# A fused cross-attention and mixture-of-experts layer: heads dealt over both halves of the rows, and a reordered head of the program

## The reference

```python
x = x + tanh(g_xattn[0]) * xattn(layernorm(x), ctx_1024, ...)   # (32, 128, 128)
x = x + tanh(g_ffn[0]) * ffn(layernorm(x), ...)

# xattn: 16 heads of width 8
qkv, qkv_a = x @ Wqkv + bqkv, xa @ Wqkv_aux + bqkv_aux
dots, dots_aux = q @ k.T * scale, q @ ka.T * scale               # the same queries, two sets of keys
p, pa = softmax(dots), softmax(dots_aux)
out = (p @ v) * (1 - sigmoid(g)) + (pa @ va) * sigmoid(g)
return out @ Wo + bo

# ffn: 64 experts of width 64, the best 8 of each token by a grouped sigmoid router, and a shared expert
y = sum over e of w[:, e] * ((silu(x @ wg[e]) * (x @ wu[e])) @ wd[e])
return y + (silu(x @ Ws_gate) * (x @ Ws_up)) @ Ws_down
```

## Time and profile before

| | |
|---|---|
| median of 3 runs | 859.26 us (859.24 to 859.61) |
| the profiled execution | 859.58 us, its span 857.8 us |
| busy, share of the span | PE 96%, weight loads 75%, DVE 80%, ACT 66%, POOL 74% |
| mean granted TensorE clock | 0.985 of 2.4 GHz |
| DMA | 120.04 MB, mean 140 GB/s |

### The profile page before, as it was taken

One profiled execution on the slowest core, in us unless ns is written; L12 is line 12 of the kernel. 1 busy time (PEld: TensorE's weight loads), 2 busy tenths in 40 slices (PEclk: granted clock), 3 DMA queues, 4 the chain that ended last, 5 costly groups with the idle time before them and its releaser, 6 DMA issues.

```text
span 857.8 us, 20206 instructions
## 1 busy us (share of the span) xinstructions
PE 826.2 (96%) x6733; PEld 646.0 (75%) x6733; DVE 683.6 (80%) x1648; ACT 566.8 (66%) x964; POOL 637.3 (74%) x602
## 2 busy tenths in 40 slices
PE   4899999999999999999999999999999999999997
PEld 3477777777766678888888888878888888888885
DVE  6789999999897769769678877867966977876665
ACT  4388888888878665575576576557557557655554
POOL 2668888888854378877787786777777788778785
PEclk8599999999999999999999999999999999999999
DMA  4677786776652167447456554654654755546562
GB/s 119 173 169 173 178 183 155 187 169 170 160 126 51 53 152 169 120 111 184 117 142 147 131 142 125 154 135 109 163 139 111 171 130 134 149 116 150 137 138 58
DMA packets 108036, 120.04 MB, mean 140 GB/s; under 512 B 28560, under 2 KB 70352, under 8 KB 106496
## 3 DMA queue, kind: packets, MB, share of 16 engines
q1 hardware_dynamic: 105056, 118.23, 57.5%
q10 hardware_dynamic: 2880, 0.59, 0.4%
HBM read 103.55 MB, written 14.71 MB: 138 GB/s over the span
## 4 chain that ended last, share of the span: by engine, by line
PE 87%; DVE 5%; DMA 3%; issue 2%; SPq 1%; ACT 1%; POOL 0%; DVEq 0%; POOLq 0%
PE bank L1999 20%; PE bank L2000 20%; PE bank L2001 20%; PE bank L1336 7%; PE bank L1323 5%; PE bank L1294 3%; PE bank L1276 2%; PE bank L1344 2%; PE bank L1260 1%; PE bank L1357 1%; DVE mx L989 1%; PE bank L1270 1%; DMA cwb<-wts_scratch 1%; DMA stack_q<-nmaxT 1%; PE bank L1976 1%
## 5 line engine op out<-in xcount | busy, mean ns | idle before, releaser
L1676 POOL TENSOR_TENSOR hid<-act,cwb 128x512 f32<-128x512 f32 x264 | 424.0, 1615 | 126.4 <-DVE act L1903 69.1
L1729 ACT ACTIVATE silu<-bank 128x512 f32<-128x512 f32 x256 | 152.9, 597 | 190.7 <-PE bank L2001 189.9
L1903 DVE TENSOR_TENSOR act<-silu,bank 128x512 f32<-128x512 f32 (+1 forms) x264 | 180.5, 684 | 119.5 <-ACT silu L1729 78.7
L1999 PE MATMUL bank<-xhi,weights_hi 128*128 128x512 f32 x520 | 206.6, 397 | 0.0
L1911 DVE TENSOR_TENSOR hlo<-hid,hhi 128x512 fp32r<-128x512 f32 x256 | 197.5, 772 | 8.5 <-ACT hhi L1735 8.3
L2001 PE MATMUL bank<-xlo,weights_hi 128*128 128x512 f32 x520 | 204.2, 393 | 0.0
L2000 PE MATMUL bank<-xhi,weights_lo 128*128 128x512 f32 x520 | 203.9, 392 | 0.0
L1735 ACT ACTIVATE hhi<-hid 128x512 fp32r<-128x512 f32 (+1 forms) x264 | 164.8, 625 | 15.7 <-POOL hid L1676 13.1
L989 DVE TENSOR_REDUCE mx<-bank 128x4 f32<-128x512 f32 x240 | 156.0, 683 | 16.6 <-PE bank L1294 14.8
L786 ACT ACTIVATE prob<-bank 128x1024 f32<-128x1024 f32 x128 | 131.2, 1025 | 48.6 <-PE bank L1323 46.5
L2001 PEld LDWEIGHTS bank<-xlo,weights_hi 128*128 128x128 f32 x520 | 97.6, 188 | 22.0
(11 more groups left out here) (238 smaller groups left out, 1022.1 us busy)
## 6 DMA issues: line engine op xcount, KB each, us to landing
cwb<-wts_scratch SPq DMA_DIRECT2D x174, 384.0 KB, 5.4
stack_k<-k_scratch SPq DMA_DIRECT2D x30, 256.0 KB, 4.3
k_scratch<-parts_k SPq DMA_DIRECT2D x15, 384.0 KB, 3.4
stack_q<-q_scratch SPq DMA_DIRECT2D x30, 128.0 KB, 2.9
stack_k<-k_scratch SPq DMA_DIRECT2D x30, 128.0 KB, 5.2
q_scratch<-parts_q SPq DMA_DIRECT2D x15, 192.0 KB, 2.7
xin<-in_x_dram SPq DMA_DIRECT2D x16, 128.0 KB, 3.0
cin<-in_ctx_dram SPq DMA_DIRECT2D x16, 128.0 KB, 3.1
```

The costliest lines, as they stand in the source:

```text
L1676: pool.tensor_tensor(h_buf[k][:], a_buf[k][:], cwb[slot][:, q % GP, :], ALU.mult).then_inc(h_ok, 1)
L1729: act.activation(s_buf[k % RS][:], g_bank[k % 2][:], ACT.Silu).then_inc(s_ok, 1)
L1903: nc.vector.tensor_tensor(a_buf[k % RS][at], s_buf[k % RS][at], u_bank[k % 3][at], ALU.mult).then_inc(a_ok, 1)
L1999: nc.tensor.matmul(bank, w[0], mh, start=first, stop=False)
```

## The change

Heads are dealt out over the two halves: head h goes to row `h % 2 * 8 + h // 2` of the 16, so even heads lie in half 0 and odd heads in half 1. The weights of the query and key projections are reordered for it (`by_row`), and the units of the scores take rows in the order `S_ROW = (0, 8, 2, 10, 4, 12, 6, 14)`, so the two units of a round lie in opposite halves. In a round TensorE issues first the eight shifted scores of both units, alternating halves and banks, then the four scores, alternating too. `stack_there` is called in round 0 alone and waits for both halves.

The biases of the projections are loaded as rows (two DMAs in place of three of single elements), reordered by ScalarE (L739 in the new file), and turned by three matmuls (L1384, `turn_biases`) and a copy. At the start, ScalarE issues three of the four pairs of key loads of chunk 0 (`load_first_k(act, ...)`), SP the others; the scores of a batch of chunk 0 wait for both halves; the first of them stand ahead of the transposes of chunk 2 on TensorE. The third split of chunk 1 moves from VectorE to GpSimd; GpSimd's clearing of the second V comes earlier, VectorE's `gate_consts` later.

```diff
-S_HEAD = (8, 10, 12, 14, 0, 2, 4, 6)
+S_ROW = (0, 8, 2, 10, 4, 12, 6, 14)
+ROW_OF = tuple(h % 2 * (H // 2) + h // 2 for h in range(H))
...
+    def load_first_q(eng, c, half):
+        wait(eng, q_first, 32)
+        eng.wait_ge(stack_clear, 2)
+        load_products(eng, q_of(0)[PARTS_AT[half]:PARTS_AT[half] + ROWS_S, :, c].rearrange("p h t -> p (h t)"),
+                      q0_v[c], False, half, HH * P, stk0[half][c])
+
+    def load_first_k(eng, c, half):
+        wait(eng, k_first[c], 16)
+        eng.wait_ge(stack_zero, 2)
+        load_products(eng, k_of(0)[PARTS_AT[half]:PARTS_AT[half] + ROWS_S, :, c].rearrange("p h a t -> p (h a t)"),
+                      k0_v[c], True, half, 2 * HH * P, stk0[half][c])
...
-        turned = lambda a: a.rearrange("(h d a) -> d h a", d=DH, a=1)
-        for i, b in enumerate((turned(v["bqkv"][0:P]), turned(v["bqkv"][P:2 * P]), turned(v["bqkv_aux"][P:2 * P]))):
-            sp.dma_start(bcol[:, i:i + 1], b, allow_slow_non_contiguous=True).then_inc(c_in, 16)
+        sp.dma_start(brow_in[:, 0:2 * P], one(v["bqkv"][0:2 * P])).then_inc(c_in, 16)
+        sp.dma_start(brow_in[:, 2 * P:3 * P], one(v["bqkv_aux"][P:2 * P])).then_inc(c_in, 16)
...
-        sp.wait_ge(stack_zero, 2)
-        sp.wait_ge(stack_clear, 2)
-        load_first(0)
+        load_first_q(sp, 0, 1)
         store_first_k(1)
-        load_first(1)
+        load_first_q(sp, 0, 0)
+        load_first_q(sp, 1, 1)
+        load_first_q(sp, 1, 0)
+        load_first_k(sp, 1, 0)
         store_q(1, 1)
...
         root(1)
+        clear_v(1)
...
-        pool.wait_ge(lo_ok, SPLITS * 2)
+        pool.wait_ge(lo_ok, SPLITS * 2 - 1)
+        split(1, 1, 1)
...
         evac_t(0, 0)
+        act.wait_ge(b_mm, 1)
+        act.activation(bcol[:], st_bank[0][:, 0:3], ACT.Copy).then_inc(b_ev, 1)
...
         copy_q(1)
         copy_k(1)
+        load_first_k(act, 0, 1)
         copy_first_ka(1)
+        load_first_k(act, 0, 0)
+        load_first_k(act, 1, 1)
...
         split(0, 0, 1, 1)
+        split(1, 1, 0, 0)
         norm_stats(2)
-        split(1, 1, 0, 0)
+        split(1, 1, 1, 0)
         norm(2)
-        gate_consts()
-        split(1, 1, 1, 0)
-        split(1, 1, 1, 1)
         for r in range(ROUNDS):
             first_maxima(0, r)
+            if r == 0:
+                gate_consts()
...
-        def stack_there(b, u):
+        def stack_there(b):
             n, c, s = b // CH, b % CH, b // CH % NST
             if c == 0:
-                wait(pe, stk[S_HEAD[u] // HH][s], 64 * ((n - 1) // NST + 1 if s else n // NST))
-            if u == 0:
-                wait(pe, shift_zero, CH if n == NST else b - CH * NST + 1)
+                for half in (1, 0):
+                    wait(pe, stk[half][s], 64 * ((n - 1) // NST + 1 if s else n // NST))
+            wait(pe, shift_zero, CH if n == NST else b - CH * NST + 1)
...
-            a, h = u % 2, (u // 2) * HPU + j
+            a, h = u % 2, ROW_OF[(u // 2) * HPU + j]
...
-            ins = nc.tensor.matmul(st_bank[u % 2][:, j * P:(j + 1) * P], k_of(n)[at, h % HH, c, a, :],
+            at_p = (a * 2 + j // 2) * P
+            ins = nc.tensor.matmul(st_bank[j % 2][:, at_p:at_p + P], k_of(n)[at, h % HH, c, a, :],
                                    q_of(n)[at, h % HH, c, :], start=True, stop=True)
-            if j == HPU - 1:
+            if a == 1 and j >= 2:
                 ins.then_inc(st_mm, 1)
...
         transposes(0, 0)
+        turn_biases()
...
+        first_scores(0, 0)
         transposes(2, 0)
-        first_scores(0, 0)
         first_scores(0, 1)
...
-                    if two_more and r % 2 == 0:
-                        stack_there(b + 2, 2 * r)
-                    for u in (2 * r, 2 * r + 1):
-                        ahead = (b + 2, u) if two_more else None
-                        shifted(b, u, 0)
-                        if ahead:
-                            scores(*ahead, 0)
-                        shifted(b, u, 1)
-                        shifted(b, u, 2)
-                        if ahead:
-                            scores(*ahead, 1)
-                        shifted(b, u, 3)
+                    if two_more and r == 0:
+                        stack_there(b + 2)
+                    u0, u1 = 2 * r, 2 * r + 1
+                    for u in (u0, u1):
+                        for j in range(HPU):
+                            shifted(b, u, j)
+                    if two_more:
+                        for j in range(2):
+                            scores(b + 2, u0, j)
+                            scores(b + 2, u1, j)
```

87 lines of the change are left out of this document (47 added, 40 removed).

## The result

The changed kernel takes 860.78 us (median of 22 runs, 858.57 to 864.77), the kernel before 859.31 (22 runs beside them): a ratio of 1.0019, 95% interval 1.001 to 1.0028, about 1.6 us slower. The time came out 0.3 us from the forecast of 860.5. The profiled execution took 860.42 us (span 858.8). So near a hit can be luck, and here it was: of the five terms of the sum only the hand-over came out as forecast. The added wait was put 2 to 3 us too high, and the loop's order and the two terms of the head were put too low by about as much together (1.1 and 1.85 us).

A forecast was written before the change was run, and what follows sets the result against it. The prediction took the loop as bound by TensorE's own order, ScalarE and VectorE just behind. Terms -1.1 + 4.7 - 1.4 - 0.45 - 0.5 summed to +1.25 us, giving 860.5 us, range 855.8 to 864.0.

The forecast's parts named there:

- the hand-over: From the last two batches to the experts: earlier exponentials shorten the router's chain, -0.5 us (0 to -0.7).
- The added wait: Even batches' first round: half 0 of the stacks is wanted 3.9 us earlier, +4.7 us (0 to +6.4).
- the loop's order: Attention loop: exponential 0.22 us earlier, first maximum 0.22 later, leaving -1.1 us over 13 pairs (0 to -3.7).
- the two terms of the head: Head: second round at 38.0 instead of 39.43, -1.4 us; first batch's third and fourth rounds, -0.45 us.
- Chunk by chunk: 0.2, 1.1, 0, 0, 0, 1.4, 0, 1.4, 0, 0.6: Delays in us from late half 0 loads for chunks 3 to 12, added up to +4.7 us.
- My walk: Pair of batches: VectorE's lateness survives as 0.07, the score behind the second maximum waits 0.18, 0.085 us gained.
- they are there by 34.9, and what comes last is the first maxima: Head: both halves of the second chunk's stacks land by 34.9 us; the first maxima, ending at 35.30, come last.
- A: Even batches' first round: loads land early enough, the added wait costs nothing, -3.4 us, 855.8 us; chance 0.22.
- B: Even batches' first round: late landings delay later chunks too, VectorE eats the loop's gain, +4.6 us, 863.9 us; chance 0.19.
- C: Loop: weight loads overlap only matmuls of another row group, so rounds shrink by 0.2 us, some 843 us; chance 0.03.
- D: Loop: two shifted scores of opposite halves hold each other up, +0.2 us per round on TensorE, 885 us; chance 0.03.
- the marks in the prediction: Trace signs: exponential 0.46 behind group, group length 0.54, first round near 35, pair near 15.5, 1 us stretches.

The follow-up runs named there:

- wait_both: The kernel before, but from the loop's second chunk on both stack halves are waited for in an even batch's first round: 861.36 us, ratio 1.002 to before.
- two_rounds: Changed kernel with second V cleared late and eight shifted scores ahead only in round 1 of even and odd batches: 859.58 us, ratio 1.0001 to before.
- before_again: The kernel before, profiled a second time without an edit; no separate median given, first expert matmul at 290.66 us.
- after_again: The changed kernel, profiled and timed a second time without an edit: 861.50 us, ratio 1.0025 to before.
- late_weights: Changed kernel with SP's loads of raw expert weights moved behind the loads of the stack's keys in the loop: 873.61 us, ratio 1.0166 to before.
- clear_late: Changed kernel with GpSimd's clearing of the second V and two small fills back behind the output weights: 861.07 us, ratio 1.0012 to before.
- head_old: Changed kernel with the old head's loads, splits, clearing and transpose order; new biases and wait for both halves stay: 864.18 us, ratio 1.0047 to before.
- best2: Changed kernel with late_weights and clear_late together, and the eight shifted scores ahead in only three rounds per pair of batches: 876.10 us, ratio 1.0186 to before.
- head_new: The kernel before with only the new head's loads, splits, clearing and score order; heads, loop, waits and biases stay: 861.88 us, ratio 1.0013 to before.

## Why the prediction was right in sum and wrong in its parts

**The added wait, +4.7: mis-sized, the term furthest off.** The mechanism was right: half 0 is late, the stretches appear, and they go into the time. wait_both prices it at 2.8 us (2.0 to 3.7), the changed kernel at 1.9 to 2.4 (its 1.6 to 2.1 us, plus the 0.4 gained at the hand-over, less 0.13 for a pair that is 0.01 longer, if the head is worth nothing), and eight traces with the wait and with the weights in their place have 0.8 to 2.1 us of stretches, two_rounds 2.3. The step that failed is "Chunk by chunk: 0.2, 1.1, 0, 0, 0, 1.4, 0, 1.4, 0, 0.6". Late landings in several chunks are not several delays. Part of the lateness is carried on from chunk to chunk (-0.34 to +2.08 in before_again); one wait gives the DMA chain that time, and the next landings are early again (0.3 to 0.6 early in the three chunks behind the 1.40 in after_again). Adding the chunks counts that part several times. The largest lateness, 1.15 in the first trace and 2.08 in the second, is nearer to what was measured, but it is no rule: in the first trace the lateness falls and rises twice, and wait_both's median price lies above both. late_weights is the opposite case: the chain's own period is longer than a pair, every chunk is late anew, and the waits add. That a carried lateness is why they don't add otherwise is argued from these traces; no run took it apart by itself.

**The loop's order, -1.1: in truth 0, out of two terms.** The pieces were seen (exponential 0.22 earlier, first maximum 0.22 later, TensorE's sum unchanged, 0.18 given back). By its own numbers the gain should have been 0.28 less 0.18, so 0.10 a pair and not 0.085. The first error is in the reading of before: of the round that "waited 0.148 for ScalarE", 0.089 was the second waiting instruction, as wait_both shows. That the change drops it is a gain of 1.1 us that I put under the exponential. The second is that the order itself costs 0.10 a pair, +1.3 us, where I had a gain. In the odd batch's round 1 the lateness from the even batch's round 3 arrives: VectorE runs without a gap from the maxima of that round to the second maximum of the odd batch, 3.7 us, and in the kernel before the score behind it started 0.17 behind its end (157.22 and 157.05 in the earlier trace rows), where 0.06 is the least seen, so 0.12 was to spare. The order shifts the two against each other by 0.30: the maxima start 0.65 behind the even round 3's group for 0.43, and TensorE goes from that group to the odd batch's round 1 in 3.98 for 4.05. Left over are 0.18, by which the second unit's score starts later in its round (0.41 for 0.23). And the late copy to `nmaxT` puts ScalarE's DMA issue and `full_q` in front of the exponential, so the 0.05 of that round's wait stayed. My walk followed the lateness into the score behind the second maximum only. two_rounds is the check: with round 3 at the old order the 0.20 is gone.

**The head, -1.4 and -0.45: in truth about 0, for reasons not in the sum.** The step "they are there by 34.9, and what comes last is the first maxima" failed twice over: the landing came at 36.16 and held the first round, and the maxima ended at 36.90 in place of 35.30 and held the second. The forecast counted GpSimd's clearing as no cost. A memset that runs on GpSimd while VectorE normalizes makes 0.60 us into 1.86; clear_late, head_old, two_rounds and best2 have 0.60, the changed kernel (twice) and the other kernels with the early clearing 1.86. The Trainium skill (SBUF — State Buffer, section "SBUF: two separate sides") has a reason: GpSimd shares a pair of ports with VectorE's operations in a two-port mode, under an exclusive lock that whichever starts first holds for the whole instruction. The trace agrees: the clearing starts 0.09 us ahead of `xn`, and `xn` ends 0.15 us behind it. No run shows in which mode `xn` ran. I also had the bias turning at nothing; it probably costs 0.5 to 0.8 at the first key split. With the clearing taken back, the first maxima end at 35.75 and the second round comes 0.75 us earlier, but the first still starts at 35.98, on the landing at 35.89. The store ahead of it came 2.4 us earlier than before (24.16 for 26.59), not 3.7. The landing of the turned maxima, at 36.11 in the changed kernel and at 37.63 in head_new, was in no term at all. What the sum did get right is that the earlier queue is needed once both halves are waited for; head_old shows what it costs without, about 2 us.

**The hand-over, -0.5: right.** From batch 30 to the first expert matmul 15.63 us against 16.04 (15.62 and 16.03 in the second profiles), -0.41.

**The rivals.** A (waits hidden) is out, B (in full) too. C (row groups) is out: the group takes 0.545 us to the next matmul, 0.547 before, so no weight load was hidden worse in one half (the odd batch's round 1, where a bank is waited for, takes 0.73). D is out: two shifted scores of opposite halves start 3 ns apart. Of the marks in the prediction, the exponential at 0.46 and the group's length held; the loop's first round near 35, the pair near 15.5 and stretches of 1 us in four or five chunks did not.

## What to carry to other kernels

Lateness seen at several steps of a chain can be one and the same lateness carried on: adding the steps up gives too much (4.7 us here, against 1.9 to 2.8) unless the chain's own period is longer than the loop's, as in late_weights. The largest lateness is a first guess of such a wait, and wants an experiment. When an order gives one engine a head start, follow the engine that it delays to the next place where it has no gap, through every queue in between, other engines' DMA issues too. When several transfers are awaited at one place, list the landing of each: with one moved, the next holds. And what changes no dependency can still cost: a second wait ahead of a critical matmul, or a memset moved to GpSimd beside a VectorE operation.

## What the runs showed of the hardware

TensorE's pace in the head is a matter of the execution, and it moves batch 1 by 0.9 us. In after_again sixteen matmuls with V at 41.86 took 1.08 us, the same sixteen at 44.02 took 0.65, and in the changed kernel's first profile they took 0.65 at 41.18:

```profile
40.71 1.22 PE L1424 MATMUL bank<-attT,ones 128*128 128x128 f32 x4
41.86 1.08 PE L1356 MATMUL bank<-prob,V 128*32 128x128 f32 x16
...
44.02 0.65 PE L1356 MATMUL bank<-prob,V 128*32 128x128 f32 x16
```

So the full pace (2.4 GHz against 1.2) was back by 42.9 in one execution and by 40.5 in the other, with the same work ahead of it: the loop's first two rounds started at 36.19 and 39.74 in the one, at 36.25 and 39.73 in the other. The granted clock doesn't tell it reliably: the stretch from 20 to 36 us reads 1.00 in before_again and 0.50 in the first profile of the same kernel (the earlier trace rows has it too), while eight scores for the maxima take 1.88 to 1.89 us in both. In the head the length of a known matmul is the better clock.

```profile
20.00:36.00 16.00, 13.10 (x49) 6.98 (x47) 14.21 (x28) 4.96 (x8) 10.45 (x22) 1.00 0.64 168
```

A waiting instruction whose semaphore has long been reached is not free: 0.089 us on TensorE where it stands beside the wait that decides (wait_both), 0.085 to 0.089 in twelve pairs alike.

And a single issue on SP can take much longer than its usual half microsecond (2.35 us for a load of weights, 2.16 for a load of keys in before_again), and holds all that is queued behind it.
